# x loaded in groups, window counts and edge gathers moved later, first mix's long stretch halved, shared tile 1 prepared sooner

## The chip, the cores and the metric

The kernel runs on one core of a Trainium2 chip. The metric is the device time of one execution in microseconds (us); the time before is the median of three runs. All figures of the trace are from one profiled execution.

## The reference, cut to what matters

Two layers of a graph network over N = 3125 nodes with 256 features and 100,000 edges that are sorted by destination.

```
xn = layernorm(x)
x  = x + GIN(xn, src, dst)                # segment sum of the sources' rows, two linear layers, batch norm
       + mix0(xn)                         # linear attention, 4 heads of 32, 4 memory keys:
                                          #   xn -> rmsnorm -> q, k, v; q softmax over its 32 features,
                                          #   k softmax over all nodes; ctx = k^T v; out = q ctx w_out + b; rmsnorm
x  = x + moe0(layernorm(x))               # 8 experts, the best 2 of each node, relu
xn = layernorm(x)
x  = x + gcn(gcn(xn)) + mix1(xn)          # two graph convolutions with edge weights; attention with instance norm
y  = layernorm(x)
x  = x + shared_expert(y) + moe1(y)       # a shared expert (256 -> 1024 -> 256, gelu) and 8 private, best 2
```

The sums over edges are done as products with an adjacency matrix. The kernel builds it in strips of 256 destinations (WG = 13 windows): for each window it finds where its edges begin in the sorted list, fetches them, and turns each edge into a key.

## The kernel before, in words

The nodes lie in T = 25 tiles of 128 rows (the last has 53), taken in G = 7 groups of four tiles (the last group is one tile). Each engine has a program of its own, written out by hand, and the engines meet through semaphores: an instruction of one engine runs in the order in which it stands there, and waits until what it needs is signalled. So the order in these programs is the schedule; nothing is reordered.

**First norm** (`first_norm_dve`, `_act`, `_pe`). DVE takes the statistics of a group (lines 495, 498, 696, 698), ACT the root, DVE its reciprocal (706, 708), ACT the normed rows XN, PE turns them (542) and DVE copies them to XT (560), PE multiplies by `gw` to q, k, v (775, 776), ACT copies these out. A group's turn is copied by DVE one group later, and at three places `lengths_dve` (723 to 735) takes the lengths for the root-mean-square norm.

**Where each window's edges begin.** Ahead of the norm: `windows_dve` (274 to 285) casts the list `first` (784 numbers, the first destination of each block of 128 edges), counts for 7 windows how many of them are smaller (277); ACT counts the other six with Sign (291). The counts give a row of `dst` for each window, which POOL gathers (13 indirect DMAs, 306). `begins_dve` (297 to 301) counts within these rows, in group 4 of the norm, and POOL gathers 13 stretches of the edges (310) into H.

**First mix** (`mix0_dve` and its like). q of a stretch of tiles loses its maximum (`q_sub_dve`, 886 and 888), the maximum of k over all nodes is taken (`k_max_dve`, 906, 909), k loses it (932), ACT takes the exponentials, PE the context, DVE divides q by its sum (`q_norm_dve`, 895 to 899). The stretches are tiles 0 to 10, 11 to 21 and 22 to 24. Between these stand the edges' steps: `places_dve` (331, the place of a destination within its window), `places_in_tiles_dve` (348, 350), `tiles_dve` (354), `keys_dve` (359), `weights_dve` (318), and PE turns the keys in four fills (`keys_pe`), which ACT copies out (`keys16_act`). Seven groups j of outputs follow (964, 967), with pieces of the first adjacency strip between them.

**Loads.** ACT's queue brings the constants CB, `first`, and x in two pieces of 12 tiles and the last tile; SP's queue brings the weights of the mix, on which the semaphore w_in counts. SP stores the normed rows to `xd` as they are formed.

**Later.** The adjacency strips and the first aggregation, moe0, the two convolutions, moe1. In the last stage 13 tiles of 256 nodes go through the shared expert (`first_*` is its first layer, `second_*` its second), and `between` puts steps of the routing between them. Every operand is split into a high and a low part: `halves_dve` (1863, 1865) splits a tile's XT, `parts_act` and `parts_dve` (1858) a weight, lines 1886 and 1888 what ACT has put out. The last group of rows is normed there too (`last_root_act`, `last_scales_dve` 2591 and 2593, `last_rows_act`, `last_turn_pe` 2537), and `warm_pe(e, 6, n)` is n pairs of idle products.

Of the kernel before, what the change touches and what calls it, by code (L numbers as in the profile page):

```python
# [14 lines left out]
N = 3125  # L15
# [24 lines left out]
W_IN = 16 * 9  # L40
# [38 lines left out]
def program(nc, ctx, a, out):  # L79
# [84 lines left out]
    firsts = WB[:, 0:784].bitcast(I32)  # L164
    firstf = WB[:, 784:1568]
    below = WB[:, 1568:1568 + WG * 392].bitcast(BF16).rearrange("p (g n) -> p g n", g=WG)
# [33 lines left out]
    def loads_act(e):  # L200
        e.dma_start(CB[:, :], a["consts"]).then_inc(S("consts"), 16)
        e.dma_start(firsts, a["first"].partition_broadcast(128)).then_inc(S("first"), 16)
        for i in range(2):
            e.dma_start(X[:, 12 * i:12 * i + 12, :],
                        a["x"][12 * i * 128:12 * (i + 1) * 128, :].rearrange("(t p) d -> p t d", p=128)).then_inc(S(f"x_in{i}"), 16)
        e.wait_ge(S("set"), 1)
        e.dma_start(X[0:LAST, T - 1, :], a["x"][(T - 1) * 128:N, :]).then_inc(S("x_in1"), 16)

    def early_sp(e):
        e.dma_start(gw, a["m_wqkv"].rearrange("(c p) n -> p c n", p=128)).then_inc(S("w_in"), 16)  # L210
        e.dma_start(cols[:, 0:16], a["cols"]).then_inc(S("w_in"), 16)
        e.dma_start(wo0, a["m_wout"]).then_inc(S("w_in"), 16)
        e.dma_start(bout0, a["m_bout"].partition_broadcast(128)).then_inc(S("w_in"), 16)
        e.dma_start(gout0, a["m_gout"].partition_broadcast(128)).then_inc(S("w_in"), 16)
# [3 lines left out]
        e.dma_start(epsc, a["eps"].partition_broadcast(128)).then_inc(S("w_in"), 16)  # L218

# [52 lines left out]
    def windows_dve(e, c):  # L272
# [3 lines left out]
        for g in range(COUNTED):  # L276
            c.add(e.tensor_scalar(below[:, g, :], firstf, w2h[:, g:g + 1], None, ALU.is_lt, ALU.add, accum_out=cnt4[:, g:g + 1]))
        c.wait()
        c.add(e.tensor_scalar(row4[:, 0:COUNTED], cnt4[:, 0:COUNTED], 1.0, 0.0, ALU.subtract, ALU.max))
        e.wait_ge(S("mix0_act"), M0A_PLACES)  # L280
# [6 lines left out]
    def windows_act(e):  # L287
        e.wait_ge(S("consts"), 16)
        e.wait_ge(S("set"), 5)
        for g in range(COUNTED, WG):  # L290
            e.activation(below[:, g, :], firstf, ACT.Sign, scale=-1.0, bias=w2h[:, g:g + 1],
                         accum_out=cnt4[:, g:g + 1]).then_inc(S("mix0_act"), 1)
# [10 lines left out]
    def windows_pool(e):  # L303
# [4 lines left out]
        e.wait_ge(S("rows"), 2)  # L308
        for g in range(WG):
# [36 lines left out]

    def places_in_tiles_dve(e, c):
        c.add(e.tensor_scalar(whii.bitcast(I32), esrc, 7, None, ALU.logical_shift_right))
# [38 lines left out]
    def keys_pe(e):  # L387
        e.wait_ge(S("wkey"), 2)
        for f in range(FILLS):
            e.wait_ge(S("lo16"), f + 1)  # L390
            turn_keys_pe(e, wkey, f, 4 + f).then_inc(S("keyT"), 1)
# [16 lines left out]
    def keys16_act(e):  # L408
        e.wait_ge(S("good"), 1)
        for f in range(FILLS):  # L410
            e.wait_ge(S("keyT"), FILLS + f + 1)
            e.activation(key2[:, windows_of(f), :], twice(fill_of(f)), ACT.Copy, scale=goodc).then_inc(S("key16"), 1)
# [182 lines left out]
    def x_added(e, k):  # L595
        def ready(t):
            if t == 0 and k == 1:
                e.wait_ge(S("x_re"), 80)
# [16 lines left out]
    class Group:  # L615
# [20 lines left out]
        def qkv(self, i):  # L636
# [10 lines left out]
              (sections[1].q(), sections[1].k(3), 22, 3)]  # L647
    sd = small[:, 300:350].rearrange("p (k t) -> p k t", k=2)
# [13 lines left out]
    M0A_PLACES, M0A_KEXP, M0A_MEM = WG - COUNTED, WG - COUNTED + 1, WG - COUNTED + 5  # L662
    M0V_W, M0V_RS, M0V_GROW, M0V_REL, M0V_KMAX, M0V_DIAG, M0V_KSUB, M0V_MEM, M0V_MASKED, M0V_CTX, M0V_CWO = (
        0, 2, 5, 6, 7, 8, 9, 13, 14, 15, 16)
# [21 lines left out]
    def first_norm_dve(e, c):  # L686
        for g in range(G):
            ts, i = tiles_of(g), g + 1
            o = slice(ts[0], ts[-1] + 1)
            if g == 0:  # L690
                e.wait_ge(S("x_in0"), 16)
                e.wait_ge(S("set"), 4)
            if g == 3:
                e.wait_ge(S("x_in1"), 32)
# [4 lines left out]
            if g == 4:  # L699
                begins_dve(e, c)  # L700
# [10 lines left out]
            if g:  # L711
                turn_dve(e, 0, g - 1)
# [2196 lines left out]
```

## Time and profile before

| | |
|---|---|
| median of 3 runs | 2214.99 us (2212.96 to 2215.39) |
| profiled execution | 2201.3 us, its span 2199.7 us |
| PE busy | 2063.6 us, 94% of the span |
| DVE busy | 1648.3 us, 75% |
| ACT busy | 1241.5 us, 56% |
| POOL busy | 594.7 us, 27% |
| moved by DMA | 338.98 MB, mean 154 GB/s |

Busy times are sums over the whole span. The stages have different limits, so shares over the span say little of one stage. PE is TensorE, DVE is VectorE, ACT is ScalarE, POOL is GpSimd, SP is SyncE; the time in a row is from the start of the span.

### The profile page before, as it was taken

The page shows a single profiled execution, that of the slowest core. Times are in us where ns is not written, and L with a number is a line of the kernel's source. Part 1 is how long each engine was busy: PE and PEld are TensorE (multiplying, and loading weights), DVE is VectorE, ACT ScalarE, POOL GpSimd, SP SyncE. Part 2 cuts the span into 40 slices and gives each one's busy share as a digit, 9 for nine tenths or more (in the row PEclk, how much of TensorE's full clock was granted, in tenths as well). Part 3 has the DMA queues.
Part 4 walks back from the last instruction along what each step waited for, and adds up shares of the span by engine and source line. Part 5 has one row for each costly group of instructions (what it writes and reads, how often), then busy time and mean ns, then how long its engine had stood idle before and what let it go on. Part 6 is the DMA issues. An engine that isn't in the chain of part 4 may idle for free. (4 is left out here: it accounts for less than half of the span.)

```text
span 2199.7 us, 46493 instructions
## 1 busy us (share of the span) xinstructions
PE 2063.6 (94%) x17860; PEld 1938.7 (88%) x17860; DVE 1648.3 (75%) x3103; ACT 1241.5 (56%) x2885; POOL 594.7 (27%) x462
## 2 busy tenths in 40 slices
PE   5769999999889999998999999999998999999996
PEld 3559999999689999997788999999998999999996
DVE  6998888885688888875657666566656868888885
ACT  6866555554547676665543444444444236767765
POOL 3100000000047777760000000000000016677774
PEclk9979999999989999999999999999999999999998
DMA  4424333344458778774004666466641026787776
GB/s 133 139 91 122 92 105 108 92 116 139 159 173 221 232 223 246 219 232 105 1 26 113 189 188 188 115 179 182 192 147 61 20 95 215 215 243 221 240 223 165
DMA packets 241142, 338.98 MB, mean 154 GB/s; under 512 B 33439, under 2 KB 202578, under 8 KB 240786
## 3 DMA queue, kind: packets, MB, share of 16 engines
q1 hardware_dynamic: 208940, 296.19, 42.5%
q0 software_dynamic: 28528, 35.76, 8.6%
q10 hardware_dynamic: 3446, 3.97, 0.6%
q8 instruction: 146, 2.39, 0.4%
q14 instruction: 82, 0.67, 0.1%
HBM read 258.89 MB, written 76.95 MB: 153 GB/s over the span
## 5 line engine op out<-in xcount | busy, mean ns | idle before, releaser
L2484 PE MATMUL bank<-WB_r,XN_r 128*128 128x448 f32 x1400 | 400.4, 367 | 0.4 <-DVE X L2261 0.4
L2017 POOL DMA_INDIRECT SC<-xd,slot_i x128 | 182.7, 1428 | 791.3 <-DVE slot_q L1653 659.8
L2419 ACT CAST WB_r<-WB 128x448 fp32r<-128x448 f32 x350 | 198.0, 567 | 248.0 <-PE bank L2484 229.3
L2424 DVE TENSOR_TENSOR WB_r<-WB,WB_r 128x448 fp32r<-128x448 f32 x350 | 217.2, 632 | 155.4 <-ACT WB_r L2419 155.0
L2484 PEld LDWEIGHTS bank<-WB_r,XN_r 128*128 128x128 f32 x1400 | 261.2, 188 | 22.6 <-DVE X L2261 0.8
L1947 PE MATMUL bank<-SC_r,WB_r 128*128 128x256 f32 (+1 forms) x2064 | 253.0, 282 | 13.2 <-issue 10.9
L1947 PEld LDWEIGHTS bank<-SC_r,WB_r 128*128 128x128 f32 x2064 | 246.3, 190 | 17.8 <-issue 17.4
L1067 ACT CAST WB_r<-bank 128x200 fp32r<-128x200 f32 x391 | 144.4, 369 | 158.9 <-PE bank L1050 158.2
L1962 PE MATMUL bank<-R_r,H_r 128*128 128x256 f32 x1752 | 215.4, 282 | 5.0 <-DVE R_r L1858 5.0
L1962 PEld LDWEIGHTS bank<-R_r,H_r 128*128 128x128 f32 x1752 | 209.1, 189 | 5.4 <-issue 5.4
L2411 POOL TENSOR_TENSOR WB<-WB,CB 128x128 f32<-128x128 f32 (+1 forms) x56 | 27.3, 488 | 610.9 <-DMA WB<-adjw 609.9
L1947 PE MATMUL bank<-SC_r,XN_r 128*128 128x256 f32 x1392 | 169.4, 280 | 4.2 <-issue 2.9
L1947 PEld LDWEIGHTS bank<-SC_r,XN_r 128*128 128x128 f32 x1392 | 164.6, 188 | 8.1 <-issue 7.7
L1819 ACT ACTIVATE yo<-yo,slot_p 128x256 f32<-128x256 f32 x118 | 53.6, 502 | 208.4 <-DVE yo L1897 203.9
L1810 ACT ACTIVATE wb_<-bank,WB 128x256 f32<-128x256 f32 (+1 forms) x344 | 133.2, 477 | 66.7 <-PE bank L1947 39.1
L2023 POOL DMA_INDIRECT slot_p<-pd,slot_q x128 | 158.8, 1240 | 41.3 <-issue 32.6
L1107 PE MATMUL bank<-H_r,WB_r 128*128 128x256 f32 x625 | 164.9, 299 | 0.0
L2484 PE MATMUL bank<-WB_r,R_r 128*128 128x448 f32 x448 | 164.4, 367 | 0.0
L1107 PE MATMUL bank<-XN_r,WB_r 128*128 128x256 f32 x625 | 153.9, 282 | 0.0
L1067 ACT COPY X<-bank 128x200 f32<-128x200 f32 x391 | 148.5, 380 | 0.0
L1023 DVE TENSOR_TENSOR SC<-R,DR 128x1024 bf16<-128x1024 bf16 x196 | 134.0, 684 | 0.0
L1107 PEld LDWEIGHTS bank<-XN_r,WB_r 128*128 128x128 f32 x625 | 118.7, 190 | 0.1
(480 smaller groups left out, 5118.7 us busy)
## 6 DMA issues: line engine op xcount, KB each, us to landing
WB<-adjw SPq DMA_DIRECT2D x350, 224.0 KB, 2.8
WB<-in_f_pack SPq DMA_DIRECT2D x127, 512.0 KB
WB<-in_f_pack SPq DMA_DIRECT2D x62, 640.0 KB
adjw<-X SPq DMA_DIRECT2D x24, 1600.0 KB, 7.8
WB<-in_f_pack SPq DMA_DIRECT2D x65, 516.0 KB
xd<-XN SPq DMA_DIRECT2D x10, 640.0 KB, 6.7
y<-X SPq DMA_DIRECT2D x10, 640.0 KB, 3.3
X<-y SPq DMA_DIRECT2D x6, 640.0 KB, 7.1
```

The lines of the kernel that those rows point to most:

```text
L1023: e.tensor_tensor(by_two(hot_lo[s][:, 0:m, :]), row(iota16, o), along(lo2, o, 128), ALU.is_equal).then_inc(S("lo1"), 1)
L1067: e.copy(to[b % 2][:, :, 8 * j:8 * j + 8].rearrange("p h (q r) -> p q h r", r=2), bank[:, :, i]).then_inc(S(name), 1)
L1107: m = e.matmul(bk[:, 0:D], CNT[b % 2][:, h, :], x[:, h * D:(h + 1) * D], start=(h == 0 and x is xnh), stop=(h == T - 1 and x is xnl), skip ...
L1810: m = e.activation(st[:, q * w:(q + 1) * w], B[hp][:, q * TS:q * TS + w], gfun[L], bias=b[:, hc:hc + 1])
L1819: e.activation(ob[:, q, :], ob[:, q, :], ACT.Copy, scale=slot_p[:, 2 * i + q:2 * i + q + 1]).then_inc(S("obs"), 1)
L1947: m = e.matmul(B[hp][:, q * TS:q * TS + w], p[:, c * HID + hc * 128:c * HID + (hc + 1) * 128], x[:, c * w:(c + 1) * w], start=(c == 0 and ...
L1962: m = e.matmul(bk[:, s * D:(s + 1) * D], x[:, hc * w + s * 128:hc * w + (s + 1) * 128], p[:, hc * D:(hc + 1) * D], start=(hc == 0 and n == ...
L2017: e.indirect_dma_start(yin[i % 2][:, q * D:(q + 1) * D], None, XD, bass.IndirectOffsetOnAxis(ap=slot_i[:, 2 * i + q:2 * i + q + 1], axis=0 ...
L2023: e.indirect_dma_start(slot_p[:, 2 * i + q:2 * i + q + 1], None, PD.rearrange("(r k) -> r k", k=1), bass.IndirectOffsetOnAxis(ap=slot_q[:, ...
L2419: e.copy(split_w(m)[0], RAW[m % PR]).then_inc(S("whigh"), 1)
L2424: e.tensor_tensor(al, RAW[m % PR], ah.bitcast(F32), ALU.subtract).then_inc(S("wlow"), 1)
L2484: mm_ = e.matmul(conv_bank(k, band, c)[:, 0:PW], x[st][:, o], y, start=(st == 0 and i == 0), stop=(st == T - 1 and i == 2))
```

## The change

**Loads.** SP's queue brings x in pieces of four tiles, tiles 0 to 3 ahead of all else, the next two pieces behind the weights that the norm needs, then `first`, tiles 12 to 23, the three weights for the outputs, the last tile. ACT's queue brings CB alone.

**Counts.** The window counts stand behind the turns of groups 1 to 4 of the norm on DVE (2, 2, 2, 1) and behind ACT's products of groups 1 to 3 (3, 2, 1). `begins_dve` moves from group 4 behind the last turn. The edge gathers also wait for the last product of q, k, v (qk), and SP's store of `xd` waits for the edges. PE does the products of group 0 ahead of the turn of group 1.

**First mix.** The second stretch is taken as 6 and 5 tiles for `q_sub` and `k_max`. `places_dve` moves from the mix's start behind the three `q_norm_dve`, and ACT's and PE's part of it follow. Keys are turned in two pairs, at j = 1 and j = 2, and all that hangs on them one j later.

**Last stage.** `halves_dve` of the next tile stands right behind the first layer, ahead of the scales of the last norm. That norm's rows are formed in tile 1, turned in tile 2, its scores follow second(1). The pairs of idle products go from 8 to 14. The routing's steps begin with tile 2.

The diff, cut to its core:

```
+    def x_tiles_sp(e, t0, t1, name):
+        e.dma_start(X[:, t0:t1, :], a["x"][t0 * 128:t1 * 128, :].rearrange("(t p) d -> p t d", p=128)).then_inc(S(name), 16)
...
     def early_sp(e):
+        x_tiles_sp(e, 0, 4, "x_in0")
         e.dma_start(gw, a["m_wqkv"].rearrange("(c p) n -> p c n", p=128)).then_inc(S("w_in"), 16)
         e.dma_start(cols[:, 0:16], a["cols"]).then_inc(S("w_in"), 16)
-        e.dma_start(wo0, a["m_wout"]).then_inc(S("w_in"), 16)
-        e.dma_start(bout0, a["m_bout"].partition_broadcast(128)).then_inc(S("w_in"), 16)
-        e.dma_start(gout0, a["m_gout"].partition_broadcast(128)).then_inc(S("w_in"), 16)
...
+        x_tiles_sp(e, 4, 8, "x_re")
+        x_tiles_sp(e, 8, 12, "x_out1")
+        e.dma_start(firsts, a["first"].partition_broadcast(128)).then_inc(S("first"), 16)
+        x_tiles_sp(e, 12, 24, "x_in1")
+        e.dma_start(wo0, a["m_wout"]).then_inc(S("x_in1"), 16)
+        e.dma_start(bout0, a["m_bout"].partition_broadcast(128)).then_inc(S("x_in1"), 16)
+        e.dma_start(gout0, a["m_gout"].partition_broadcast(128)).then_inc(S("x_in1"), 16)
+        e.wait_ge(S("set"), 1)
+        e.dma_start(X[0:LAST, T - 1, :], a["x"][(T - 1) * 128:N, :]).then_inc(S("x_in1"), 16)
...
+    COUNTS_DVE = {1: range(0, 2), 2: range(2, 4), 3: range(4, 6), 4: range(6, COUNTED)}
+    COUNTS_ACT = {1: range(COUNTED, 10), 2: range(10, 12), 3: range(12, WG)}
...
         e.wait_ge(S("rows"), 2)
+        e.wait_ge(S("qk"), T)
         for g in range(WG):
             e.indirect_dma_start(h_all[:, 384 * g:384 * (g + 1)].bitcast(I32), None, a["edges"].rearrange("(r k) -> r k", k=3),
...
-            if g == 4:
-                begins_dve(e, c)
...
             if g:
                 turn_dve(e, 0, g - 1)
+            if g == 1:
+                firsts_dve(e)
+            if g in COUNTS_DVE:
+                counts_dve(e, c, COUNTS_DVE[g])
+            if g == 4:
+                windows_dve(e, c)
         q_sub_dve(e, c, 0)
         k_max_dve(e, c, 0)
         turn_dve(e, 0, G - 1)
+        begins_dve(e, c)
...
     def mix0_dve(e, c):
-        places_dve(e, c)
-        q_sub_dve(e, c, 1)
-        k_max_dve(e, c, 1)
-        k_max_dve(e, c, 2)
+        for i in (1, 2):
+            q_sub_dve(e, c, i)
+            k_max_dve(e, c, i)
+        k_max_dve(e, c, 3)
...
-        q_norm_dve(e, c, 0)
-        places_in_tiles_dve(e, c)
-        good_dve(e)
+        for i in range(3):
+            q_norm_dve(e, c, i)
+        places_dve(e, c)
...
     def sp_program(e):
         early_sp(e)
         e.wait_ge(S("qk"), T)
+        e.wait_ge(S("edges"), 16 * WG)
         store_sp(e, XD, XN, "xd_out", xn_ready(e, 0))
```

In `dve_program`, and behind it in `pe_program`, the last stage:

```
         def tile(i):
+            if i == 2:
+                last_turn_dve(e, G - 1)
             first_dve(e, 1, NSLOT + i, shared_w(i))
+            if i + 1 < SHT:
+                halves_dve(e, shared_x(i + 1), NSLOT + i + 1, shared_w(i + 1))
             if i == 0:
-                last_scales_dve(e, G - 1)
                 parts_dve(e, 1, 1, SHARED)
             if i == 1:
-                last_turn_dve(e, G - 1)
-            if i + 1 < SHT:
-                halves_dve(e, shared_x(i + 1), NSLOT + i + 1, shared_w(i + 1))
+                last_scales_dve(e, G - 1)
...
             if i == 0:
-                warm_pe(e, 6, 8)
+                warm_pe(e, 6, 14)
```

How the orders moved, at three places.

DVE at the program's start. WB and R are the buffers of `first`; line 277 (now 286) is a count, line 495 (now 511) the statistics of a tile. Before, seven counts stand ahead of the first statistics:

```order
L274 CAST WB<-WB 128x784 [waits first]
L277 TENSOR_SCALAR WB,small<-WB,CB 128x784 [waits set]
L277 TENSOR_SCALAR WB,small<-WB,CB 128x784 x6
L279 TENSOR_SCALAR small<-small 128x7 [waits chain]
L281 TENSOR_SCALAR small<-small 128x6 [waits mix0_act]
L283 TENSOR_SCALAR small<-small 128x6 [waits chain]
L285 CAST small<-small 128x13 [waits chain]
L495 BN_STATS small<-X 128x6 [waits set,x_in0]
```

In the changed kernel the first counts stand behind group 1, and group 2 follows them:

```order
L727 RECIPROCAL small<-small 128x4 [waits std]
L729 SCALAR_TENSOR_TENSOR small<-small 128x4 [waits norm]
L576 COPY XT<-bank 128x512 [waits xT]
L281 CAST R<-R 128x784 [waits first]
L286 TENSOR_SCALAR H,small<-R,CB 128x784 [waits set]
L286 TENSOR_SCALAR H,small<-R,CB 128x784
L511 BN_STATS small<-X 128x6 [waits x_out1]
```

The first statistics now wait for x's first piece alone, and the statistics of group 2 stand behind a cast and two counts.

DVE where the norm passes into the mix. Before, the last turn (560) is followed by the places (331), which wait for the edges, and then by the second stretch of q (886):

```order
L906 TENSOR_REDUCE small<-wide_wb 128x128 [waits chain,qkv]
L560 COPY XT<-bank 128x128 [waits xT]
L716 TENSOR_SCALAR small<-small 128x25
L718 MEMSET wide_wb 128x22
L718 MEMSET wide_r_53 128x3
L331 TENSOR_SCALAR H<-H,CB 128x128 [waits edges]
L331 TENSOR_SCALAR H<-H,CB 128x128 x11
L331 TENSOR_SCALAR H<-H,CB 128x128 [waits chain]
L886 TENSOR_REDUCE small<-wide_wb 128x44 [waits qkv]
```

Now the begins (307), which wait for the gathered rows of `dst`, stand behind the last turn (576), and the halved stretch (918) behind them:

```order
L938 TENSOR_REDUCE small<-wide_wb 128x128 [waits chain,qkv]
L576 COPY XT<-bank 128x128 [waits xT]
L307 TENSOR_SCALAR DR,small<-R,CB 128x128 [waits drow]
L307 TENSOR_SCALAR DR,small<-R,CB 128x128 x12
L309 SCALAR_TENSOR_TENSOR small<-small 128x13 [waits chain]
L311 CAST small<-small 128x13 [waits chain]
L744 TENSOR_SCALAR small<-small 128x25
L746 MEMSET wide_wb 128x22
L746 MEMSET wide_r_53 128x3
L918 TENSOR_REDUCE small<-wide_wb 128x24 [waits qkv]
```

The wait for the rows of `dst` has come into the place where the wait for the edges was, and the edges are asked for only there.

DVE in the last stage, from the last split of tile 0's hidden layer (1888, now 1921) to the first of tile 1 (1886, now 1919). R_r_57 is a weight of the second layer, SC_r_59 the split input of tile 1. Before:

```order
L1888 TENSOR_TENSOR H_r_49<-wb_,H_r_49 128x512 [waits hh]
L2591 RECIPROCAL small<-small 128x4 [waits std]
L2593 SCALAR_TENSOR_TENSOR small<-small 128x4 [waits norm]
L1858 TENSOR_TENSOR R_r_57<-WB,R_r_57 128x1024 [waits w2h] x2
L1863 CAST SC_r_59<-XT 128x512 [waits h1]
L1865 TENSOR_TENSOR SC_r_59<-XT,SC_r_59 128x512 [waits xs]
L1886 CAST DR_r_56<-wb_ 128x512 [waits act1,y2]
```

And now:

```order
L1921 TENSOR_TENSOR H_r_49<-wb_,H_r_49 128x512 [waits hh]
L1896 CAST SC_r_59<-XT 128x512 [waits h1]
L1898 TENSOR_TENSOR SC_r_59<-XT,SC_r_59 128x512 [waits xs]
L1891 TENSOR_TENSOR R_r_57<-WB,R_r_57 128x1024 [waits w2h] x2
L1919 CAST DR_r_56<-wb_ 128x512 [waits act1,y2]
```

Tile 1's split stands ahead of the weight's, and the scales have gone behind the first layer of tile 1.

## Rows read from the trace of the kernel before

**Rows 1.** Windows: stretch, length, busy of PE, PEld, DVE, ACT, POOL, PEclk, DMA share, GB/s

```profile
0.00:20.00 20.00, 0.00 (x0) 0.00 (x0) 10.68 (x27) 7.73 (x14) 0.19 (x4) 1.00 0.74 239
...
54.00:132.00 78.00, 50.78 (x285) 39.58 (x283) 73.79 (x180) 60.40 (x133) 6.72 (x6) 0.90 0.45 134
180.00:1640.00 1460.00, 1416.87 (x12385) 1322.12 (x12382) 1060.22 (x1995) 795.78 (x1941) 295.09 (x242) 0.99 0.52 153
```

**Rows 2.** Timeline of DVE, first norm: start, duration, line, [idle before <-releaser]

```profile
8.55 1.03 DVE L277 TENSOR_SCALAR_CACHE_REDUCE WB<-WB,CB 128x784 bf16<-128x784 f32 x1
...
19.76 1.41 DVE L495 BATCH_NORM_STATS2 small<-X 128x6 f32<-128x256 f32 x4
...
22.96 1.39 DVE L495 BATCH_NORM_STATS2 small<-X 128x6 f32<-128x256 f32 x4
...
36.77 1.40 DVE L495 BATCH_NORM_STATS2 small<-X 128x6 f32<-128x256 f32 x4
...
38.77 0.34 DVE L297 TENSOR_SCALAR_CACHE_REDUCE DR<-R,CB 128x128 f32<-128x128 int32 x1
...
44.85 1.39 DVE L495 BATCH_NORM_STATS2 small<-X 128x6 f32<-128x256 f32 x4
```

**Rows 3.** DMA issues of the page: count, KB each, median us to landing

```profile
X<-in_x ACTq DMA_DIRECT2D x2, 1536.0 KB, 12.2
...
CB<-in_consts ACTq DMA_DIRECT2D x1, 360.5 KB, 3.8
...
H<-in_edges,small POOLq DMA_INDIRECT x13, 3.1
```

**Rows 4.** Timeline of POOL: first and last of the 13 edge gathers

```profile
43.00 0.94 POOL L310 DMA_INDIRECT H<-in_edges,small  x1 [6.73 <-DVE small L301]
...
58.00 2.27 POOL L310 DMA_INDIRECT H<-in_edges,small  x1 [0.30 <-issue]
```

**Rows 5.** Timeline of DVE, from the norm's end through the first mix

```profile
57.82 1.62 DVE L888 TENSOR_TENSOR wide_wb<-wide_wb,small 128x1408 f32<-128x1408 f32 x1
...
62.87 3.04 DVE L331 TENSOR_SCALAR H<-H,CB 128x128 f32<-128x128 int32 x13 [0.47 <-DMA H<-in_edges,small]
65.81 1.61 DVE L886 TENSOR_REDUCE small<-wide_wb 128x44 f32<-128x1408 f32 x1
...
83.89 1.37 DVE L348 TENSOR_SCALAR wide_wb<-H 128x1664 int32<-128x1664 int32 x1
...
88.89 0.17 DVE L940 RECIPROCAL small<-bank 128x1 f32<-128x1 f32 x1 [0.99 <-PE bank L790]
...
94.11 1.60 DVE L895 TENSOR_REDUCE small<-wide_wb 128x44 f32<-128x1408 f32 x1
...
99.06 0.32 DVE L318 SCALAR_TENSOR_TENSOR wide_wb<-H 128x128 f32<-128x128 f32 x1
```

**Rows 6.** Costliest groups of the page: gathers of moe0 and moe1, busy and mean ns

```profile
L2017 POOL DMA_INDIRECT SC<-xd,slot_i x128 | 182.7, 1428 | 791.3 <-DVE slot_q L1653 659.8
```

**Rows 7.** Timeline of PE, last stage: tile 0, the idle products, tile 1

```profile
1658.09 5.84 PE L1947 MATMUL bank<-SC_r,WB_r 128*128 128x256 f32 x48 [0.68 <-issue]
1663.77 1.95 PE L576 MATMUL bank<-CB 128*128 128x128 f32 x16
1670.82 8.00 PE L1947 MATMUL bank<-SC_r,WB_r 128*128 128x256 f32 x48 [5.10 <-issue]
```

**Rows 8.** Timeline of DVE, last stage

```profile
1665.69 0.69 DVE L1888 TENSOR_TENSOR H_r<-wb_,H_r 128x512 fp32r<-128x512 f32 x1
...
1670.03 0.69 DVE L1865 TENSOR_TENSOR SC_r<-XT,SC_r 128x512 fp32r<-128x512 f32 x1
```

**Rows 9.** Window of tile 1's first products

```profile
1670.00:1675.00 5.00, 4.18 (x19) 4.21 (x20) 0.69 (x1) 1.70 (x2) 0.00 (x0) 0.50 0.31 105
```

**Rows 10.** Timeline: first slot gather on POOL, and PE's turn of its rows

```profile
1782.69 1.01 POOL L2017 DMA_INDIRECT SC<-xd,slot_i  x1 [145.91 <-DVE slot_q L1653]
...
1816.28 0.60 PE L1974 MATMUL bank<-CB,SC 128*128 128x128 f32 x4
```

More of the change, by code:

```diff
@@ L39 @@
 SHT = 13
-W_IN = 16 * 9
+W_IN = 16 * 6
 W_LATE = 16 * 8
@@ L285, in windows_dve, with windows_act @@
         e.tensor_copy(row4i, row4).then_inc(S("rows"), 1)
-    def windows_act(e):
-        e.wait_ge(S("consts"), 16)
+    def windows_act(e, gs):
         e.wait_ge(S("set"), 5)
-        for g in range(COUNTED, WG):
+        for g in gs:
             e.activation(below[:, g, :], firstf, ACT.Sign, scale=-1.0, bias=w2h[:, g:g + 1],
@@ L385, in places_pe, with keys_pe @@
             turn_keys_pe(e, wlo, f, 4 + f).then_inc(S("keyT"), 1)
-    def keys_pe(e):
+    def keys_pe(e, half):
         e.wait_ge(S("wkey"), 2)
-        for f in range(FILLS):
-            e.wait_ge(S("lo16"), f + 1)
-            turn_keys_pe(e, wkey, f, 4 + f).then_inc(S("keyT"), 1)
+        for f in (2 * half, 2 * half + 1):
+            if half:
+                e.wait_ge(S("key16"), f - 1)
+            else:
+                e.wait_ge(S("lo16"), FILLS)
+            turn_keys_pe(e, wkey, f, 6 + f % 2).then_inc(S("keyT"), 1)
     def total_pe(e):
@@ L406, in keys_act, with keys16_act @@
             e.copy(lo2[:, windows_of(f), :], twice(fill_of(f))).then_inc(S("lo16"), 1)
-    def keys16_act(e):
+    def keys16_act(e, half):
         e.wait_ge(S("good"), 1)
-        for f in range(FILLS):
+        for f in (2 * half, 2 * half + 1):
             e.wait_ge(S("keyT"), FILLS + f + 1)
-            e.activation(key2[:, windows_of(f), :], twice(fill_of(f)), ACT.Copy, scale=goodc).then_inc(S("key16"), 1)
+            e.activation(key2[:, windows_of(f), :], twice(part_of(f)), ACT.Copy, scale=goodc).then_inc(S("key16"), 1)
     def turn_weights_pe(e, f):
@@ L647, in program @@
               (sections[1].q(), sections[1].k(3), 22, 3)]
+    q_all, k_all = sections[0].q(), sections[0].k(22)
+    stretches = [(q_all[:, a0:a0 + n, :], k_all[:, a0:a0 + n, :], a0, n) for a0, n in ((0, 11), (11, 6), (17, 5))] + groups[2:]
+    SUBTRACTED = (1, 3, 4)
     sd = small[:, 300:350].rearrange("p (k t) -> p k t", k=2)
@@ L752, in first_norm_act @@
                 first_products_act(e, t)
+            if g in COUNTS_ACT:
+                windows_act(e, COUNTS_ACT[g])
     def first_products_act(e, t):
@@ L760, in first_norm_pe @@
     def first_norm_pe(e):
-        for g in range(G):
+        turn_pe(e, 0, 0)
+        first_products_pe(e, 0)
+        turn_pe(e, 0, 1)
+        for g in range(2, G):
             turn_pe(e, 0, g)
-            if g:
-                first_products_pe(e, g - 1)
+            first_products_pe(e, g - 1)
         first_products_pe(e, G - 1)
@@ L901, in k_max_dve @@
     def k_max_dve(e, c, i):
-        _, k, t0, n = groups[i]
+        _, k, t0, n = stretches[i]
         to = kmore if i else km
```

109 lines of the change are left out of this document (56 added, 53 removed).

## The prediction, made before the changed kernel ran

> **What bounds the kernel now.** I read the windows first, because the kernel has stages with different limits. From 54 to 132 us DVE is busy 73.79 of 78.00 us while PE is busy 50.78; from 180 to 1640 us PE is busy 1416.87 of 1460.00 at a granted clock of 0.99 [rows 1]. So what the change gives at the front is what it brings DVE forward until PE takes over, and it keeps its worth from there, since PE's long stretch has its order unchanged and starts as soon as the first strips are there. Second, DVE's timeline at the start: the first statistics begin at 19.76, behind seven counts of which the first begins at 8.55 [rows 2]. The DMAs carry 239 GB/s over the first 20 us [rows 1], and x's large pieces take 12.2 us from issue to landing [rows 3], so x comes no sooner than some 14 us as it is asked for now. Third, DVE's timeline of the mix: it waits 0.47 us for the edges at 62.87 and 0.99 us for PE at 88.89, and otherwise runs through [rows 5]. Fourth, the last stage: between tile 0's first products with their idle products behind them and tile 1's, PE is idle 5.10 us, and tile 1's 48 products take 8.00 us where tile 0's took 5.84 [rows 7]; the window shows a clock of 0.50 there [rows 9], which is 1.2 GHz, behind an idle engine.
>
> All sums are made against the profiled execution, 2201.3 us with a span of 2199.7. The median of the runs, 2214.99, lies 13.7 us above it; I take differences from the trace and set them against the median.
>
> **The front, step by step.** x's first four tiles are 0.5 MB, asked for at once beside the constants (0.36 MB, landed 3.8 us after their issue [rows 3]). The two are 0.9 MB, 3.7 us at 239 GB/s; with the start and the latency I take 6.1 us for the landing. Bounds: as soon as the constants, about 5; or 8 if the weights behind share the bandwidth. Group 1's statistics came 3.2 us behind group 0's [rows 2], so now at about 9.5. To group 4's it was 36.77 − 22.96 = 13.8 us. Into these come the cast of `first` (0.6) and six counts at 0.95 (0.95 is the pitch, the row's 1.03 overlaps the next), 6.3 together, less 0.6 of waits that they fill: group 4 begins at 29.0 instead of 36.77. From there before to group 5's statistics was 8.1 us with 3.9 of begins in it [rows 2]; without them 4.2, plus one count 0.95, the root's wait 1.0 that the begins hid, and 0.8 for the rows' numbers: these are formed at 36.0.
>
> Now the gathers of `dst`. They used to lie far ahead of their reader and now they do not. 13 of them run at a pitch of (58.00 − 43.00)/12 = 1.25 us [rows 4], so the last starts at 36.3 + 15.0 = 51.3 and lands 3.1 us later [rows 3], at 54.4. One thing speaks against that pitch: the last gather of before took 2.27 us where the first took 0.94 [rows 4], and it ran beside DVE's subtraction of 1.62 us at 57.82, which reads two inputs from SBUF [rows 5]. The new gathers run beside one such subtraction, so 1.3 more: 55.7, say 56. DVE comes to the begins at 52 (from group 5's statistics at 44.85 to 62.40 were 17.5 us, less some 1.5 of waits for roots that now are there) and waits 4 us. The begins end at 59.9 and the mix starts at 60.1; before it stood at that point at 62.87 − 0.47 = 62.40. **The start is 2.3 us ahead**, of the 10 by which x came sooner: 4 are left at the new wait, the begins (3.9) still stand in the way, having only changed places.
>
> The mix behind it: the 0.99 us at 88.89 closes, since the context is long done when DVE, with three `q_norm` and the places first, comes to it; the stretch in two pieces costs one more set of three operations and a maximum, about 0.75 by the fixed part of such operations (0.55 for 384 elements against 1.6 for 1408, so about 0.15 each, and the maximum 0.3). That is +0.25, so 2.55 ahead. Then the edges. Their gathers start at 60.2 behind the begins, by now also behind the last q, k, v, which are done by then (PE begins some 10 us sooner). 13 at 1.25 with the stretching: in this stretch lie some 9 us of DVE operations with two inputs. As a mean over many gathers, the slots' gathers take 1.43 us each beside such work [rows 6], 0.48 more than 0.95; 13 × 0.4 gives about 5 us. The last starts at 80.2 and lands 3.1 to 4.9 us later (62.87 less 58.00 is 4.9), at 83.3 to 85.1. DVE wants them at 60.1 + 18.1 (65.81 to 83.89) + 5.0 (94.11 to 99.06) + 0.75 = 84.0 [rows 5]. A stall of 0 to 1.1, I take 1.0. **Front: 2.55 − 1.0 = 1.5 us.** Bounds: with no stretching at all 1.3 + 1.0 more, and with x at 5 instead of 6.1 one more, 4.8; with x and `first` late by 2 each −2. SP's store of `xd` now waits for the edges, but its reader stands behind the whole mix, so I cost it at nothing; keys turned in pairs one j later only move work between groups that have DVE as their bound: nothing, and 1 us if a group of outputs waits for ACT's copies.
>
> The Trainium skill, SBUF — State Buffer, section "Who interferes with whom", says that a DVE `tensor_tensor` takes only the shared pair's read interface, that descriptor generation needs the write interface, and that a probe showed no stalling of DMA by it (it calls the reason inferred). By that rule the stretching would be gone and the front worth 3.8 instead of 1.5. The row of 2.27 us beside the subtraction speaks against it.
>
> **The last stage.** DVE's last split of tile 0's hidden layer ends at 1665.69 + 0.69 = 1666.38, and tile 1's split came after scales and a weight's split, ending at 1670.72 [rows 8]. Now the 1.11 us of tile 1's split follow at once, and PE starts tile 1 at 1667.5 instead of 1670.82: 3.3 us. The 14 pairs take 1.95 × 14/8 = 3.4 us, from 1663.77 to 1667.2, so PE is idle for only 0.3 us and the 48 products run at the clock of 1.0 (2.4 GHz): 8.00 − 5.84 = 2.2 us. The weight's split is needed by second(0) at 1673.3 and ends at 1669.9. The turn of the last rows behind second(0) may wait 0.3 us for them. **Last stage: 3.3 + 2.2 − 0.3 = 5.2 us.** Bounds: 3.3 if the clock stays low, 5.7 with no wait. The routing begins about 6 us later on the clock of the stage; the slots' first gather goes from 1782.69 to about 1788, its rows are wanted by PE at 1816.28 − 5.2 = 1811 [rows 10], and a gather lands in under 5 us: hidden.
>
> Sum: 1.5 + 5.2 = 6.7 us, 2201.3 to 2194.6, and on the median 2215.0 to **2208.3**.
>
> **Rivals.**
> (a) The gathers are not stretched, or x comes still sooner: front 3.8 to 4.8, total −9 to −10, about 2205.5. For it: the pitch was 1.25 for twelve of thirteen gathers. Against: the one beside the two-input operation.
> (b) The front gives nothing or loses 2: the chain counts → `dst` gathers → begins → edge gathers → places is now in series with DVE, and each late microsecond of x or `first` passes through. Total −5.2 to −3.2, about 2211.5, within what can't be told. For it: of 10 us that x gains, 8 are already lost in my own sum. If x's pieces all land together at 17.6 instead of in order, group 1 comes 11 us later, the 4 us of DVE's wait move with the rows, and the front loses about 8: total +3, also near no change.
> (c) Slower: the gathers at a slow pitch p. The last `dst` row lands at 39.5 + 12p and the begins end at 43.4 + 12p, the edges land at 46.7 + 24p, and are wanted 23.8 after the mix's start. The front's gain is 19.0 − 12p, less 12p − 20.7 where that is positive. At 1.73 (1.43 and the 0.30 between gathers [rows 4, 6]) it is −1.8; at 2.3 it is −15.5, total +10, 2225. It decides at p = 2.06, where the loss of 9.6 outweighs the last stage by 0.2%. Against: DVE would have to run two-input operations nearly all the time; during the `dst` gathers it runs small ones and copies from PSUM, beside which twelve gathers kept their pitch.
> (d) The last stage gives only its 3.3 or its 2.2: total −3.7 to −4.8, around 2211.
>
> **How the numbers follow.** About 0.2% (4.4 us) is what a measurement of this kernel can tell from no change. My forecast, 2204 to 2210.5, gets 0.48; (a) 0.16; (b) and (d) together 0.26; (c), with any mishap of its kind, 0.10. Faster by over 0.2% takes the forecast, (a) and a little of (b): 0.66; within it the rest of (b) and (d): 0.24; slower 0.10. The range reaches from (a) to the weak end of (b): 2203 to 2214.
>
> **What the changed profile would show.** Statistics of group 0 at 6 to 7 and of group 4 near 29; the first `dst` gather at 36; a wait of DVE for R<-in_dst of about 4 us before the begins; the mix's q_sub of the second stretch at 60; a wait of under 1 us or none at the places near 84; the first strip's work some 1.5 us sooner; in the last stage no idle of 5 us between tile 0 and 1 and a clock of 1.0 there. The prediction is wrong if group 0 waits for x beyond 8, if the gathers have a pitch above 1.7, if DVE stalls for edges by more than 3 us, or if PE's long stretch doesn't start sooner by what DVE gains.

## The result, and the profile after

The changed kernel takes 2195.35 us (median of 3 runs, 2194.43 to 2196.06) against 2214.99: ratio 0.9918, 95% interval 0.9902 to 0.9933. That is 19.6 us faster where I had forecast 6.7. The two profiled executions, however, differ by what I had summed: spans of 2199.7 and 2194.5, 5.2 us apart. So the 13 us that I missed are not between the two traces; they are between the trace of before and its own median. The two traces are also not of one kind: the first has all 208 landing signals of each series of 13 gathers, the changed kernel's has 49 (dst) and 95 (edges). What goes with that, runs 1, 2 and 13 to 15 show.

The windows of the changed kernel (columns as in [rows 1]):

```profile
54.00:132.00 78.00, 45.56 (x254) 37.60 (x254) 71.39 (x202) 57.82 (x128) 15.92 (x16) 0.80 0.53 155
180.00:1640.00 1460.00, 1416.22 (x12374) 1321.28 (x12373) 1059.42 (x1993) 795.17 (x1937) 297.75 (x242) 0.99 0.52 153
1665.00:1670.00 5.00, 4.51 (x39) 4.34 (x39) 4.43 (x7) 2.32 (x5) 0.00 (x0) 1.00 0.00 0
1670.00:1675.00 5.00, 5.00 (x46) 5.00 (x45) 4.25 (x9) 3.74 (x7) 0.00 (x0) 1.00 0.01 2
```

DVE is still the bound of the mix, and PE's long stretch is what it was. In the last stage PE runs through, at the full clock; in [rows 9] it stood at 0.50.

DVE's timeline of the changed kernel, first norm and mix:

```profile
6.11 1.40 DVE L511 BATCH_NORM_STATS2 small<-X 128x6 f32<-128x256 f32 x4 [0.94 <-DMA X<-in_x]
9.41 1.40 DVE L511 BATCH_NORM_STATS2 small<-X 128x6 f32<-128x256 f32 x4
...
30.57 1.40 DVE L511 BATCH_NORM_STATS2 small<-X 128x6 f32<-128x256 f32 x4
...
57.36 0.35 DVE L307 TENSOR_SCALAR_CACHE_REDUCE DR<-R,CB 128x128 f32<-128x128 int32 x1 [2.66 <-DMA R<-in_dst,small]
...
61.36 0.94 DVE L918 TENSOR_REDUCE small<-wide_wb 128x24 f32<-128x768 f32 x1
...
84.57 3.01 DVE L342 TENSOR_SCALAR H<-H,CB 128x128 f32<-128x128 int32 x13
...
95.16 0.16 DVE L416 TENSOR_SCALAR small<-bank 128x1 f32<-128x1 f32 x1 [0.84 <-PE bank L412]
```

The norm starts 13.65 us sooner than in [rows 2], and the mix's second stretch comes at 61.36 where before the places stood ready at 62.40 [rows 5]: a lead of 13.65 has shrunk to 1.0, as forecast in kind. The places at 84.57 wait for nothing.

POOL's timeline: the gathers of dst, then of the edges:

```profile
37.89 1.12 POOL L316 DMA_INDIRECT R<-in_dst,small  x1 [37.14 <-DVE small L296]
...
49.34 1.98 POOL L316 DMA_INDIRECT R<-in_dst,small  x1 [0.30 <-issue]
...
54.13 0.94 POOL L316 DMA_INDIRECT R<-in_dst,small  x1 [0.30 <-issue]
61.60 0.94 POOL L321 DMA_INDIRECT H<-in_edges,small  x1 [6.53 <-DVE small L311]
...
77.68 0.94 POOL L321 DMA_INDIRECT H<-in_edges,small  x1 [0.30 <-issue]
```

PE's timeline of the last stage, beside [rows 7]:

```profile
1657.58 5.84 PE L1980 MATMUL bank<-SC_r,WB_r 128*128 128x256 f32 x48 [0.77 <-issue]
1663.26 3.29 PE L592 MATMUL bank<-CB 128*128 128x128 f32 x28
1667.04 5.84 PE L1980 MATMUL bank<-SC_r,WB_r 128*128 128x256 f32 x48 [0.49 <-issue]
```

Tile 1 follows tile 0 by 9.46 us instead of 12.73, and its 48 products take 5.84 instead of 8.00.

### The profile page after: what moved, and what is told of

Same layout as the page of the kernel before. It is cut to its first block and busy times, and to the rows that moved or that the text cites. A ratio compares the mean times of both kernels' runs of the same rounds, so it can differ in the third digit from the quotient of the medians.

```text
span 2194.5 us, 46527 instructions
## 1 busy us (share of the span) xinstructions
PE 2068.3 (94%) x17872; PEld 1940.9 (88%) x17872; DVE 1648.0 (75%) x3107; ACT 1239.5 (56%) x2884; POOL 599.1 (27%) x462
## 5 line engine op out<-in xcount | busy, mean ns | idle before, releaser
L2056 POOL DMA_INDIRECT slot_p<-pd,slot_q x128 | 164.1, 1282 | 39.0 <-issue 37.5
```

The source lines that it names most:

```text
L2056: e.indirect_dma_start(slot_p[:, 2 * i + q:2 * i + q + 1], None, PD.rearrange("(r k) -> r k", k=1), bass.IndirectOffsetOnAxis(ap=slot_q[:, ...
```

## The experiments

All were timed against the kernel of before on the same chip. Runs 1 to 4 were taken on one chip, 5 to 8, 9 to 12, 13 to 15 and 16 to 18 on another each; so a time in us compares best within such a set, and across sets the ratio to before does. In a row, `<-remote` marks a wait whose end the profile can't put down to work that had just ended, `<-issue` idle time for which it shows no wait.

**1 and 2: both kernels again.** No edit.

> The kernel of before, unchanged, against itself. In the two profiles the change gives 5.2 us (spans of 2199.7 and 2194.5), in the medians 19.6 (2214.99 and 2195.35). Theory A: the changed kernel is worth what the profiles show, about 5 us, and the median of before was high because those runs were taken on another chip or under other conditions: this kernel then gives a span and a time within some 2 us of the 'before' of this call, and both stand 4 to 7 us above the changed kernel of this call. Theory B: the kernel of before really takes about 2215 in most executions and 2201 only in some; its runs here then spread between 2201 and 2215, and the profiled ones with a long span show where the 14 us lie.

> The changed kernel, unchanged, against the kernel of before on the same chip. Theory A: ratio 0.997 to 0.998, 5 to 7 us faster. Theory B: ratio near 0.991, 19 us faster, and the changed kernel's own runs lie close together at 2194 to 2197.

Measured: before again 2212.62 (12 runs, 2207.36 to 2216.51), ratio 0.9995 (0.9986 to 1.0004), and the 23 runs of before beside it 2213.25 (2209.22 to 2217.41). The changed kernel 2194.36, ratio 0.9918 (0.9906 to 0.993). Theory A falls. None of these 35 executions came down to the 2201.3 that I had read. This time the profiled one has a span of 2214.9. DVE's and ACT's timelines of it:

```profile
33.52 0.36 DVE L498 BATCH_NORM_AGGREGATE small<-small 128x2 f32<-128x6 f32 x4
36.59 0.17 DVE L696 TENSOR_SCALAR small<-small 128x4 f32<-128x4 f32 x1 [2.70 <-remote]
...
66.01 0.69 DVE L560 COPY XT<-bank 128x512 f32<-128x512 f32 x1 [3.58 <-remote]
```

```profile
38.75 1.52 ACT L757 ACTIVATE wide_wb<-bank,small 128x384 f32<-128x384 f32 x3 [5.04 <-PE bank L776]
...
56.81 0.58 ACT L757 ACTIVATE wide_wb<-bank,small 128x384 f32<-128x384 f32 x1 [0.79 <-PE bank L776]
59.67 0.58 ACT L757 ACTIVATE wide_wb<-bank,small 128x384 f32<-128x384 f32 x1 [2.27 <-PE bank L776]
...
65.95 0.58 ACT L550 COPY XT<-bank 128x512 f32<-128x512 f32 x1 [4.58 <-remote]
```

and POOL's and PE's:

```profile
20.35 1.11 POOL L306 DMA_INDIRECT R<-in_dst,small  x1 [19.60 <-DVE small L285]
...
35.54 0.94 POOL L306 DMA_INDIRECT R<-in_dst,small  x1 [0.31 <-issue]
47.53 0.94 POOL L310 DMA_INDIRECT H<-in_edges,small  x1 [11.04 <-DVE small L301]
...
62.51 0.95 POOL L310 DMA_INDIRECT H<-in_edges,small  x1 [0.31 <-issue]
```

```profile
54.04 0.81 PE L776 MATMUL bank<-wb_,XT 128*128 128x384 f32 x2
...
55.33 0.81 PE L776 MATMUL bank<-wb_,XT 128*128 128x384 f32 x2
...
62.01 0.38 PE L542 MATMUL bank<-CB,XN 128*128 128x128 f32 x2
67.16 1.62 PE L775 MATMUL bank<-wb_,XT 128*128 128x384 f32 x2 [4.77 <-ACT wide_wb L757]
```

What the reader is to see: DVE at 36.59 waits for its own aggregate, done at 33.9; ACT and DVE at 66 wait for PE's turn, done at 62.4. The work was there and the signal was not. Twice this lasts until the end of a series of gathers (the last ones issued at 35.54 and 62.51, some 3 us before; the last landing signals stand at 38.74 and 65.93). It begins well ahead of the end: the products that ACT copies at 56.81 and 59.67 were done at 54.85 and 56.14, the first of them 7.3 us behind the edges' first gather. In the series of dst the first late one was done at 31.83, 11.5 us behind the first gather. Instruction by instruction against the first trace of before, this execution is 0.2 us late up to 33, 4.5 at 40, 9.9 at 70, and 10.5 at 90 to 150; the rest of its 15.2 comes later, 3.2 of it behind the first products of the last stage (1670.07 against 1658.09). The page too tells the two traces apart: [rows 3] has a time to landing for the edge gathers, this page has none, as only 37 of their 208 landing signals stand in the trace (all 208 in the first).

```profile
R<-in_dst,small POOLq DMA_INDIRECT x13
H<-in_edges,small POOLq DMA_INDIRECT x13
```

**3 and 4: the change's two halves alone.** Run 3 has only the diff's last stage (the second fence of the diff and `between`), run 4 all the rest.

> The kernel of before with the last stage of the change alone. Theory A: 4.9 us faster by the traces (PE's first turn of slot rows went from 1816.28 to 1810.85, of which 0.5 came from ahead of the stage), ratio 0.9975 to 0.998. Theory B with the cost at the start: the same 4.9 us and the rest of the 19 us missing. Theory B with the cost in the last stage: about 19 us, ratio 0.991.

> The kernel of before with the front of the change alone (loads, counts, gathers, first mix), the last stage as before. Theory A: 0.5 to 1.0 us faster by the traces (first work of the last stage 1658.09 before and 1657.58 after), no difference that can be measured, ratio 0.9992 to 1.0000. Theory B with the cost at the start: about 14 to 15 us faster, ratio 0.993. My prediction's sum for this part was 1.5 us.

Measured: last stage 2207.89, ratio 0.9979 (0.997 to 0.9987), 5.4 us (4.6 by the ratio); front 2200.22, ratio 0.9941 (0.9926 to 0.9955), 13.0 us. The missed gain comes with the front's part of the change.

**5 and 6: the edge gathers in and out of the norm.** Both have before's loads, counts and begins and the change's mix; run 5 holds the edge gathers back, run 6 does not.

```
         e.wait_ge(S("rows"), 2)
+        e.wait_ge(S("qk"), T)
```

> The kernel of before with its own loads, counts and begins, and the change's first mix: places behind the three q_norm, edge gathers behind the last product of q, k, v. Theory S (late signals): engines' semaphore signals come 3 to 5 us late while a series of 13 indirect gathers ends under the first norm; the repeated run of before loses 4.3 us at 34 to 38 (gathers of dst) and 5.5 us at 60 to 66 (gathers of the edges). Here only the first is left: 4 to 5.5 us faster than before, ratio 0.9975 to 0.998, and no wait of ACT or DVE of over 3 us at 60 to 66. Rival R (the 10 us come from something else at the start, such as the large loads or the counts): within 1 us of before, ratio near 1.000.

> The same without the wait for the last product, so that the edges are gathered under the norm as before. Theory S: both delays are there again, within 1 us of before, ratio 0.999 to 1.000, some 4 to 5 us slower than the kernel with the wait. Rival R: no difference between the two but for the edges' earlier landing, this one up to 1 us faster.

Measured: with the wait 2208.46, ratio 0.9971 (0.9959 to 0.9983); without it 2212.8, ratio 0.9995 (0.9986 to 1.0005). The two kernels differ by this one line, and it is worth 4.3 us (5.3 by the ratios). In run 5 the first delay is there, and at 60 to 66 no wait of 3 us and more stands; in run 6 both are there. DVE, run 5, then run 6:

```profile
37.05 0.17 DVE L705 TENSOR_SCALAR small<-small 128x4 f32<-128x4 f32 x1 [3.49 <-remote]
...
90.62 3.00 DVE L332 TENSOR_SCALAR H<-H,CB 128x128 f32<-128x128 int32 x13 [2.11 <-DMA H<-in_edges,small]
```

```profile
37.84 0.17 DVE L704 TENSOR_SCALAR small<-small 128x4 f32<-128x4 f32 x1 [3.53 <-remote]
...
67.34 0.16 DVE L714 RECIPROCAL small<-small 128x1 f32<-128x1 f32 x1 [12.76 <-ACT small L750]
```

The second row of run 5 is the price, a wait for the edges that are now late by 2.1. Where run 6 waits 12.76 us, run 5 waits 3.06 and the first trace of before 4.13.

**7: the changed kernel with x loaded as before.**

```
+        e.dma_start(firsts, a["first"].partition_broadcast(128)).then_inc(S("first"), 16)
+        for i in range(2):
+            e.dma_start(X[:, 12 * i:12 * i + 12, :],
+                        a["x"][12 * i * 128:12 * (i + 1) * 128, :].rearrange("(t p) d -> p t d", p=128)).then_inc(S(f"x_in{i}"), 16)
-        x_tiles_sp(e, 0, 4, "x_in0")
...
```

> The changed kernel with x loaded as before (two pieces of 12 tiles behind the constants and first on ACT's queue, all weights on SP's). My sum: the first statistics wait for x until 14.2 us instead of 6.1, and since the counts, the gathers and the begins stand in series with DVE all 8 us pass through: 2202, ratio 0.9955 against before. Rival: the wait of 3 to 4 us for the rows of dst takes up part of it, a loss of 4 to 5 us only, ratio 0.9935 to 0.994.

Measured: 2203.94, ratio 0.9953 (0.994 to 0.9966), 10.0 us faster than before, and 8 to 9 slower than the changed kernel, whose gain was 18 to 20 us on other chips. The times alone would hardly exclude the rival, since the two intervals are 3 us wide to either side; the trace does. The first statistics begin at 14.46 instead of 6.11, the first gather of dst at 45.90 instead of 37.89, the first of the edges at 69.66 instead of 61.60, and DVE waits 2.77 us for the rows of dst where the changed kernel waited 2.66. What x comes later passes through.

**8: the counts sooner.**

```
-    COUNTS_DVE = {1: range(0, 2), 2: range(2, 4), 3: range(4, 6), 4: range(6, COUNTED)}
+    COUNTS_DVE = {1: range(0, 4), 2: range(4, COUNTED)}
```

with ACT's as {1: three, 2: three} and `windows_dve` in group 3.

> The changed kernel with the counts in groups 1 and 2 (DVE 4 and 3, ACT 3 and 3), the gathers' rows formed in group 3 instead of 4. DVE waits 3 to 4 us at 20 for a turn, which two of the counts can fill. By the chain alone the gathers of dst start at about 31 instead of 38, land at 51, and DVE's wait of 2.7 to 4 us for them is gone: 3 to 4 us faster than the changed kernel, ratio 0.990 against before. Theory S: the end of the series (45 to 51) now falls under the last products of the norm, where signals come late: 0 to 3 us faster than the changed kernel, with waits of ACT or DVE of 2 us and more for signals at 45 to 52.

Measured: 2199.29, ratio 0.993 (0.9917 to 0.9943), some 3 to 5 us slower than the changed kernel, though its gathers begin 7 us sooner. POOL, DVE and ACT of it:

```profile
30.95 1.12 POOL L316 DMA_INDIRECT R<-in_dst,small  x1 [30.19 <-DVE small L296]
...
46.16 0.95 POOL L316 DMA_INDIRECT R<-in_dst,small  x1 [0.30 <-issue]
```

```profile
47.36 0.69 DVE L576 COPY XT<-bank 128x512 f32<-128x512 f32 x1 [6.39 <-issue]
```

```profile
49.55 2.00 ACT L787 ACTIVATE wide_wb<-bank,small 128x384 f32<-128x384 f32 x4 [6.00 <-remote]
```

By pulling the series back under the norm the delay is back too, and larger than I had allowed (I had expected 0 to 3 us of gain). PE had done the turn for which DVE waits until 47.36 at 40.66, 9.7 us behind the series' start.

**9 and 10: a pause in the series.** In run 9 the kernel of before, in both series; in run 10 the kernel of run 8, in the series of dst.

```
         for g in range(WG):
+            if g == 7:
+                e.wait_ge(S("drow"), 16 * 7)
```

The series of the edges in run 9 has the same on its own semaphore, `edges`.

> The kernel of before, with one pause in each series of 13 gathers: POOL waits for the landing of the first seven before it issues the other six. The late signals began some 13 us after a series had started (20.35 to 33.5, 47.5 to 60.8) and lasted until it had landed. Theory S1 (a backlog that grows along the series): the pause lets it drain, the waits of 3 to 6 us at 34 and 60 are gone, at the price of some 2.5 us of later edges: 7 to 10 us faster than before, ratio 0.9955 to 0.997. Theory S2 (signals are late at the end of a series whatever stands ahead of it): no faster, or 1 to 3 us slower by the pauses, ratio 1.000 to 1.0015.

> The changed kernel with the counts sooner (which was 5 us slower than the changed kernel, with waits of 6 us at 41 to 49) and the same pause in the series of dst. S1: the waits of 6 us are gone and the chain's gain remains, 2 to 4 us faster than the changed kernel, ratio 0.9895 to 0.991, and 7 to 9 faster than without the pause. S2: as without the pause, ratio 0.993 to 0.9945.

Measured: 2207.22, ratio 0.9971 (0.9962 to 0.9981), 6.3 us faster than before; a little under the 7 to 10 that I had put; and 2190.52, ratio 0.9897 (0.9881 to 0.9912), 8.8 us less than run 8 and 3.8 less than the changed kernel's 2194.36, both of other chips (7.3 and 4.6 by the ratios). S2 falls. In run 9 ACT's waits of 5.04 and 4.58 and DVE's of 2.70 and 3.58 of run 1 are gone. What is left is DVE's wait for ACT's root at 56.37 (5.15, where the first trace of before has 4.13) and one of ACT of 1.98 at 54.72, when only seven gathers had been issued. The pauses and the edges' landing cost what was expected; POOL and DVE:

```profile
30.98 0.94 POOL L308 DMA_INDIRECT R<-in_dst,small  x1 [1.75 <-DMA R<-in_dst,small]
...
55.39 0.94 POOL L314 DMA_INDIRECT H<-in_edges,small  x1 [2.24 <-DMA H<-in_edges,small]
```

```profile
37.25 0.18 DVE L710 RECIPROCAL small<-small 128x4 f32<-128x4 f32 x1 [2.62 <-issue]
...
56.37 0.16 DVE L710 RECIPROCAL small<-small 128x1 f32<-128x1 f32 x1 [5.15 <-ACT small L746]
...
66.44 3.02 DVE L335 TENSOR_SCALAR H<-H,CB 128x128 f32<-128x128 int32 x13 [1.63 <-DMA H<-in_edges,small]
```

**11: the second stretch whole.** The changed kernel with `stretches = groups`, one `q_sub` and one `k_max` for it.

> The changed kernel with the mix's second stretch taken whole (11 tiles) again. q, k and v of all tiles are there at 58 while DVE comes to the stretch at 61, so by the trace the split brings nothing and costs about 0.75 us: 0 to 1 us faster than the changed kernel, ratio 0.991 to 0.992. Rival: ACT's exponentials and the context start sooner by the split, this one 1 to 2 us slower.

Measured: 2194.94, ratio 0.9914 (0.9898 to 0.9929): no difference that can be measured. In its trace DVE is 1.7 us further ahead at 110 than in run 2, 1.0 of which it had already at 50, ahead of the stretch; the 0.7 that are left fit the 0.75 that I had put on the split.

**12: eight idle pairs.** `warm_pe(e, 6, 14)` behind tile 0 back to 8.

> The changed kernel with 8 pairs of idle products in the last stage instead of 14. PE is then idle for 1.8 us ahead of tile 1 (1665.2 to 1667.0) instead of 0.5. If the granted clock falls to half as it did behind 5.10 us of idle, tile 1's 48 products take 8.0 instead of 5.84 us: 2.2 us slower than the changed kernel, ratio 0.993. If 1.8 us of idle leave it at full, no difference, ratio 0.992, and the six more pairs were worth nothing.

Measured: 2197.07, ratio 0.9926 (0.9912 to 0.994), 1.8 us over the changed kernel by the two ratios, whose intervals overlap, and 2.1 over run 11 on the same chip. So the time alone doesn't tell it from no difference; the trace does. PE, and the window of it:

```profile
1662.04 1.95 PE L592 MATMUL bank<-CB 128*128 128x128 f32 x16
1665.82 7.40 PE L1980 MATMUL bank<-SC_r,WB_r 128*128 128x256 f32 x48 [1.83 <-issue]
```

```profile
1665.00:1670.00 5.00, 4.18 (x24) 4.21 (x25) 4.07 (x5) 1.10 (x3) 0.00 (x0) 0.69 0.01 2
```

Behind 1.83 us of idle PE ran part of tile 1 at half clock: 7.40 us instead of 5.84. In steps of 1 us the clock is 0.95 from 1666 to 1667 and 0.50 in the three behind it.

**13 to 15: how short a series, and the changed kernel's own.** Run 13 is before with pauses at g in (4, 8) in both series, run 14 is run 10 with the stretch whole, run 15 the changed kernel with one pause in the series of dst.

> The kernel of before with two pauses in each series of gathers, after the fourth and the eighth. If even a run of seven already makes signals late, shorter ones remove the rest of the 10 us (the wait of 2.6 us at 37), at the price of one more pause of 1.75 to 2.2 us ahead of the edges' landing, for which DVE already waited 1.6 us: between 1 us faster and 2 us slower than with one pause, ratio 0.9965 to 0.998. If seven are short enough, the second pause only costs its 2 us: ratio 0.998.

> The changed kernel with the counts sooner, one pause in the series of dst, and the second stretch whole. The three edits lie at different places: 3.8 us from the first two as measured together, and 0 to 1 us from the whole stretch, since DVE comes to it now at 56 while the last product ends at about 51: 2189.5 to 2190.5, ratio 0.989 to 0.9897.

> The changed kernel with one pause in the series of dst, nothing else. Its own late signals (ACT's wait of 3.45 us for PE at 51, in the repeated run) would go, but the rows of dst, for which DVE waits 4 us anyway, land some 1.75 us later: 0 to 2 us slower than the changed kernel, ratio 0.992 to 0.993. If the late signals also held up the gathers' own landing, it is as fast or up to 2 us faster.

Measured: 2208.44, ratio 1.0031 (1.002 to 1.0042); 2191.3, ratio 0.9951 (0.9938 to 0.9964); 2194.86, ratio 0.9971 (0.9962 to 0.9981). None of the ratios fits its expectation, and the reason is the kernel of before beside them: it took 2201.29 here (18 runs, 2197.59 to 2206.57), on a chip that no earlier run had had. On it the pauses only cost: run 13 is 7.1 us slower than before, with waits of DVE for the gathers in place of any late signal:

```profile
41.32 0.35 DVE L297 TENSOR_SCALAR_CACHE_REDUCE DR<-R,CB 128x128 f32<-128x128 int32 x1 [2.28 <-DMA R<-in_dst,small]
```

Run 15's trace has none of ACT's wait of 3.45 us at 51 of run 2, and 5.22 us of DVE's wait for dst instead of 3.97. All three traces have all 208 landing signals of each series, as has the first trace of before; the sixteen others have 36 to 95 of 208 for a series under the norm. The questions of these three runs were thus not answered as put; what they showed is that the chips differ.

The missing records are not a matter of these series alone. Over the whole kernel the sixteen traces hold 76 to 79% of all landing signals, the other four 99%. So signals come late on the chips on which their records are lost, and which of the two brings the other, if either does, is not shown. Every timed execution of this case has a span and a granted clock on record, so each was watched by the profiler, and no run tells whether an execution without it has late signals too. Each chip also appears in one set of runs alone: what differs may be the chip or something else of that set.

**16 to 18: once more, on a fifth chip.** The changed kernel, its front alone (run 4) and run 10.

> The changed kernel, unchanged, with the kernel of before beside it on the same chip. If before takes about 2201 there (signals in time): 5 to 7 us faster, ratio 0.997 to 0.9975, as my prediction's sum of 6.7 had it. If before takes about 2213 (signals late): 18 to 19.5 us faster, ratio 0.9912 to 0.992, as in the calls before. A ratio between these would speak against a difference of two kinds of chip.

> The front of the change alone. Signals in time: 0 to 1.5 us faster than before, ratio 0.9993 to 1.000. Signals late: 13 us faster, ratio 0.994.

> The changed kernel with the counts sooner and one pause in the series of dst: 2190 to 2191.5 on either kind of chip, 3 to 4 us faster than the changed kernel beside it.

Measured: before 2215.99; changed 2194.6, ratio 0.99 (0.9884 to 0.9915); front 2202.71, ratio 0.9944 (0.993 to 0.9958), 13.3 us; run 10's kernel 2192.66, ratio 0.9893 (0.9875 to 0.9911), 1.9 us under the changed kernel here. The front came as expected. The changed kernel gained 21.4 us, 2 more than I had put for late signals, with the interval just reaching the expected ratios; run 10's kernel was 1 us above its range, and its lead of 1.9 instead of 3 to 4 is one that these few runs hardly tell from none. Four of the five chips had late signals. On the one without, the changed kernel itself did not run; the nearest is run 15, 6.4 us faster than before there.

## Why the prediction was wrong, by its own steps

**The step that failed** is the one on the sum's footing: "The median of the runs, 2214.99, lies 13.7 us above it; I take differences from the trace and set them against the median." The 13.7 us were the clue. In the trace of run 1, which does belong to such a median, 10.3 us are late signals under the norm, which the change touches and which the trace that I had doesn't show (offset 10.5 at 90 less 0.2 at 30); the rest lies elsewhere and no run says what it is. The sum put this at nothing, and a range laid around the median couldn't reach it. Nor did a sign of being wrong that I had named come up in the trace: x at 6.11, pitches of 1.35, no stall for the edges. On the trace that I had, the sum held: 6.7 forecast, 5.2 between the spans, though these are of two kinds of chip, and 6.4 for run 15 on the one chip whose before is 2201.

**The front**, forecast 1.5, measured 13.0 and 13.3 on chips with late signals. The edges' series leaves the norm: 4.3 us (runs 5 and 6). The series of dst stays under it, but from 38 to 55 instead of 20 to 36, when DVE, which sets the end, waits for that very series: ACT's wait of 3.45 us is covered. The rest of the delay at 34, 4.3 us, is thus spared as well. That this accounts for it is argued from the traces; run 8, where the series slid back and 6 us of waits appeared, and run 10, where a pause removed them, show the mechanism. Then there is the lead by x, the 1.0 us of the pair of traces. Together these are 9.6 of the 13.0. The first products of the last stage come 11.2 us sooner in run 4 than in run 1 (1658.86 against 1670.07), and the spans differ by 13.9 (2201.0 and 2214.9), so some 3 us arise behind them, where both kernels have the same order. Why is open.

**x in groups**: landing at 6.1 was right to the row, and so was "each late microsecond passes through" (run 7: 8 us later, 8 to 9 slower).

**The chain**: group 4 at 30.57 (forecast 29.0), a turn waited 2.83 us for PE at 22.9 that I had put at nothing; gathers at 37.9 (36.3); one stretched by 1.04 (1.3); DVE's wait 2.66 (4); the mix at 61.36 (60.1). **The edges**: I put 5 us on the stretching of their series by two-input operations; it was 77.68 − 61.60 = 16.08 for twelve pitches, 1.1 over 15.0, though some 8 us of such operations ran beside it, 3.16 of them in one stretch at 72.14. (By my own 0.48 a gather the term would even have been 6, not 5.) The mean of [rows 6] was the wrong row for it; the Trainium skill's rule (SBUF — State Buffer, "Who interferes with whom"), by which these operations don't hold up the making of descriptors, came nearer, though not the whole way: the gather at 49.34 beside DVE's subtraction took 1.98. So DVE waited 0 instead of 1.0 at the places. A new wait of 0.84 at 95.16, for PE's count that had moved behind the context, took that back. So the front's 1.0 against a forecast of 1.5 is in part luck: a chain that was 1.3 us late and an edges' term that was too large by 4 us, of which only 1.0 had been set to count, lie on opposite sides.

**The last stage**: 5.2 forecast, 4.9 in the traces (the turn of the first slot at 1810.85 against 1816.28 [rows 10], less the 0.5 us that tile 0 was sooner), 5.4 in run 3. Its parts held: 3.27 us sooner by the split (3.3), 5.84 instead of 8.00 by the clock (2.2). **Slots, store of xd, keys in pairs**: the first slot gather came at 1788.09 (forecast 1788); none of the three was run alone.

**Rivals**: (c), slow gathers, needed a pitch of 2.06; the two series of the changed kernel had 1.35 and 1.34. (a) comes nearest in direction, not in reason: its gathers were hardly stretched, but that gave 1.0 us and not 13. (d) falls, both halves of the last stage came.

## What to carry to other kernels

Where a trace's own time lies outside the spread of the runs beside it, it is not a trace of what is timed: the gap is a cost to be found before any sum, or the range has to reach over it. Where signals come late as here, a long series of indirect gathers doesn't belong under a stretch in which engines hand small pieces to one another; put it beside long instructions, or where the reader waits anyway, or break the series. An edit that removes such waits is worth different times on different chips (two pauses cost 7.1 us where signals were in time), so compare on one, and see whether the trace has all its landing signals.

## What the runs showed of the hardware

On four chips of five, engines waited 3 to 6 us for signals of work long done while a series of 13 indirect gathers (128 descriptors each) ran towards its end; even an engine's own signal to itself came late (DVE, 2.70 us). Both kinds of series have it, 64 KB and 192 KB a gather, but it doesn't set in at one time. The first work whose signal was late ended 9.7 us (run 8), 11.5 us (run 1) and 13.0 us (run 3) behind the start of the series of dst, and 5.9 us (run 6) and 7.3 us (run 1) behind that of the edges. The 13 us that I put in both series ahead of run 9 is thus too long for the edges, and the bytes aren't ruled out. A pause of about 2 us after the seventh gather removed most of it (runs 9 and 10). On the fifth chip the kernel of before took 2201.29, and the traces of runs 13 to 15 show none. What queues up, and why the chips differ, stays open.

The clock of TensorE: behind 0.49 us of idle PE stayed at full speed (1.00), behind 1.83 us (run 12) it went on at full speed to 1667 and then fell to 0.50, behind 5.10 us it stood at 0.50 in tile 1's first products [rows 9].
